# First attention of a two-layer transformer kernel: one pass of scores, with probability rows scaled, turned on TensorE and copied, in place of a second pass over keys

## The chip, the cores and the metric

The kernel runs on one core of a Trainium2 chip. The metric is the device time of one execution in microseconds (us), the median of several. The engines are TensorE (PE in the profile; its weight loads are PEld), VectorE (DVE), ScalarE (ACT), GpSimd (POOL) and SyncE (SP, which here issues all DMAs). They run their own instruction queues in order and meet at semaphores.

## The reference

A batch of 16 sequences of 512 tokens and 128 features goes through two layers. All of it is f32. Both layers have attention and an FFN in parallel on the same input.

```python
# layer 0 attention: 16 heads of 64, ALiBi slopes, causal
q, k, v = split(x @ w_qkv)
sim = einsum('bhid,bhjd->bhij', q * 64 ** -0.5, k)
sim = sim - abs(j - i) * slopes[h]
sim = where(causal, mask_value, sim)
attn = softmax(sim, axis=-1)
out = (attn @ v) @ w_out + b_out
# layer 0 and 1 FFN: LayerNorm twice, dequantised 128 -> 512 -> 128, GELU-like gate, residual
# layer 1 attention: differential, 16 sub-heads of 8, RoPE, no mask, per-head RMS norm
```

## The kernel before

The work of one batch element is cut into **ticks**; a **body** is 32 ticks, and in every body 8 pairs of heads of the first attention are started, one every 4 ticks (a **step**). The other parts of an element hang on a table of tick numbers (`X_AT` to `OUT_AT`, lines 98 to 111), counted from the element's first tick; an element lives for more than three bodies, so a body works on several elements at once. `pipeline` (line 528) writes bodies -1 to 2, a hardware loop of 12 turns over one body for elements 3 to 14, and bodies 15 to 17. Each engine has its own `body` that lists its instructions tick by tick; no engine waits for a tick, they only wait on semaphores, so a queue runs ahead or behind as its semaphores allow.

**First attention**, for a pair `p` of heads `j` = 0, 1, one on each half of the partitions. TensorE projects q, k and v (`project_q` and its like); ScalarE and VectorE split q and k into a high and a low f32r part (`QH`, `QL`, `KH`, `KL`). `max_scores0` (line 1325) makes the scores with queries on partitions, one 128-row block `q` per tick, three matmuls for each head. VectorE's `row_max0` (line 1071) adds the relative positions and the mask (`relkey`), takes the row maximum into `mx0` and throws the sum itself away (`junk`). A tick set later (`pair(s, 1)`) the maxima are turned (`minus_max`, line 1322), split by ScalarE (line 807) and VectorE (line 1042), and SP copies them by four small DMAs into rows of `QM` (line 571). Then `key_scores0` (lines 1358, 1361) makes the same scores again with **keys** on partitions: three matmuls for the products, one for positions and maxima (`KM`, `QM`), and two bf16 matmuls for the mask (`maskb`), for each head and block of keys. ScalarE's `exp0` (line 854) takes the exponential into `pt`. `pv0` (line 1375) multiplies with v; ScalarE copies the result into `att` (line 831). GpSimd adds the blocks of `pt` (`add_probs`, lines 703 and 707); every second step `sums0` (line 1384) sums them over partitions, ScalarE copies (line 838), SP spreads them over partitions (line 580), VectorE inverts (line 1080), SP writes them to HBM and reads them back as a broadcast into `rbc` (lines 585, 591), and GpSimd multiplies `att` by it (`normalise`, line 715). `attention_out` (line 1394) follows twice per element.

**Second attention** runs from tick `L1_AT` in 45 chunk steps over 28 ticks. `rotate` (VectorE, lines 1093 to 1105) makes three bf16 parts of q and of k; SP's `stack` writes them to HBM (line 600), 64 partitions at a time, and reads them back as stacks (line 606), which `s_stk` reports. Scores with queries on partitions (line 1442) give maxima on VectorE (line 1125), which go as rows through SP (line 615); scores with keys on partitions (line 1435) give exponentials on ScalarE (line 877), and line 1404 multiplies with v.

**Banks.** All score tiles of both attentions (`mx0`, `st0`, `mx1`, `st1`) take turns in five PSUM banks in the order that `score_order` writes down; before it writes a bank, TensorE waits until the tile that was there five places earlier has been read (`bank_free`): by VectorE for `mx0` and `mx1`, by ScalarE for `st0` and `st1`. All other TensorE results take turns in two banks (`pj_order`).

## Time and profile before

| | |
|---|---|
| median of 3 runs | 3957.96 us (3951.04 to 3959.59) |
| profiled execution | 3963.12 us, of which the span from first to last instruction is 3961.3 us |
| TensorE busy | 3169.1 us (80%), 20864 matmul records, mean granted clock 0.873 |
| VectorE busy | 2004.2 us (51%) |
| ScalarE busy | 1558.8 us (39%) |
| GpSimd busy | 1073.6 us (27%) |
| DMA | 105.81 MB, 27 GB/s on average |

Matmul ends are modelled, and a record lasts longer than the distance to the next one, so costs in a dense row of matmuls are read from start to start. In a view of waits "issue" means that the profile shows nothing that the engine waited for.

### The profile page before, as it was taken

To read this page: it belongs to the slowest core of one execution; us is meant where nothing else is said; L and a number is where in the kernel's file an instruction comes from. 1 tells how busy PE (TensorE), PEld (TensorE's weight loads), DVE (VectorE), ACT (ScalarE), POOL (GpSimd) and SP (SyncE) were. 2 spreads that over 40 slices of the span, in tenths; PEclk is the share of its full clock that TensorE was granted. 3 is DMA by queue.
4 is the path that set the end of the run, shared out by engine and by line. 5 is a ranking of instruction groups with operands and counts; after the bars stand their busy time and mean duration, and the time that the engine had idled before them with its cause. 6 is when DMAs were issued, how large, how long until landed. Compare 5 with 4: busy or idle time off the path is not lost. (4 is left out here: it accounts for less than half of the span.)

```text
span 3961.3 us, 67447 instructions
## 1 busy us (share of the span) xinstructions
PE 3169.1 (80%) x20864; PEld 1662.4 (42%) x20864; DVE 2004.2 (51%) x5450; ACT 1558.8 (39%) x3241; POOL 1073.6 (27%) x1482
## 2 busy tenths in 40 slices
PE   4877878788787887878878788787878878788767
PEld 2544444444444444444444344443444444444422
DVE  3345455455545554554555555545545555455455
ACT  2433434334343343534434344343443434344344
POOL 1432232323223232232322313222132231323120
PEclk9998889888798888988989889888988989889886
DMA  2010020100101001010010101101010020100120
GB/s 65 18 39 20 10 47 13 42 16 15 41 16 41 13 15 41 16 47 8 20 37 16 47 8 39 24 10 47 8 47 16 10 47 13 44 13 13 41 46 4
DMA packets 102986, 105.81 MB, mean 27 GB/s; under 512 B 35524, under 2 KB 81988, under 8 KB 99404
## 3 DMA queue, kind: packets, MB, share of 16 engines
q1 hardware_dynamic: 102604, 101.07, 10.6%
q8 instruction: 196, 3.21, 0.3%
q14 instruction: 186, 1.52, 0.1%
HBM read 68.77 MB, written 29.88 MB: 25 GB/s over the span
## 5 line engine op out<-in xcount | busy, mean ns | idle before, releaser
L1125 DVE TENSOR_REDUCE mx<-sc 128x1 f32<-128x512 f32 x1024 | 642.4, 679 | 251.7 <-PE sc L1442 250.8
L854 ACT ACTIVATE pt<-sc 128x512 f32<-128x512 f32 (+3 forms) x1024 | 392.2, 435 | 765.9 <-PE sc L1361 764.9
L877 ACT ACTIVATE pt<-sc 128x512 f32<-128x512 f32 x1024 | 555.8, 602 | 340.4 <-PE sc L1435 339.9
L1071 DVE CUSTOM_DVE_ANT_0 junk<-sc,relkey 128x128 bf16<-128x128 f32 (+3 forms) x1024 | 464.3, 487 | 370.0 <-PE sc L1337 236.0
L1442 PE MATMUL sc<-KS,QS 48*128 48x512 bf16 x1024 | 287.1, 433 | 317.7 <-issue 187.1
L703 POOL COPY psums<-pt 128x128 f32<-128x128 f32 x256 | 74.7, 295 | 1331.2 <-ACT pt L854 1331.0
L1276 PE MATMUL pj<-xnT,wqkv 128*128 128x512 f32 x512 | 376.3, 826 | 44.5 <-ACT y L800 37.6
L707 POOL TENSOR_TENSOR psums<-psums,pt 128x256 f32<-128x256 f32 (+1 forms) x512 | 306.8, 622 | 334.8 <-ACT pt L854 334.8
L707 POOL TENSOR_TENSOR psums<-pt 128x384 f32<-128x384 f32 x256 | 252.3, 1007 | 507.8 <-ACT pt L854 506.6
L1435 PE MATMUL sc<-QS,KS 51*128 51x512 bf16 x1024 | 262.7, 415 | 133.7 <-DVE mx L1071 109.6
L1358 PE MATMUL sc<-QH,KH 64*128 64x256 f32 (+2 forms) x1024 | 281.6, 434 | 89.1 <-DVE mx L1071 54.6
L1375 PE MATMUL pj<-pt,v 128*64 128x512 f32 (+3 forms) x2048 | 351.4, 489 | 0.6
L1404 PE MATMUL op<-pt,v 128*32 128x512 f32 x2048 | 318.1, 697 | 31.1 <-ACT pt L877 30.2
L1375 PEld LDWEIGHTS pj<-pt,v 128*64 128x64 f32 x2048 | 151.1, 153 | 310.4 <-issue 271.5
L1337 PE MATMUL sc<-KH,QH 64*128 64x256 f32 (+2 forms) x1024 | 258.8, 453 | 23.4 <-DVE mx L1125 20.6
L1442 PEld LDWEIGHTS sc<-KS,QS 48*128 48x128 bf16 x1024 | 68.2, 96 | 493.8 <-issue 233.8
L1028 DVE SCALAR_TENSOR_TENSOR y<-tanh,y 128x512 f32<-128x512 f32 x128 | 95.2, 744 | 336.5 <-ACT y L800 336.3
L819 ACT ACTIVATE KH<-pj 128x512 fp32r<-128x512 f32 x128 | 76.4, 597 | 466.7 <-PE pj L1276 465.7
L1358 PEld LDWEIGHTS sc<-QH,KH 64*128 64x128 f32 x1024 | 134.1, 195 | 263.1 <-DVE mx L1125 100.7
L1435 PEld LDWEIGHTS sc<-QS,KS 51*128 51x128 bf16 x1024 | 64.9, 95 | 420.0 <-issue 200.8
L1358 PE MATMUL sc<-QL,KH 64*128 64x256 f32 (+2 forms) x1024 | 217.1, 352 | 0.0
L1358 PE MATMUL sc<-QM,KM 64*128 64x256 f32 (+2 forms) x1024 | 204.9, 340 | 0.0
(130 smaller groups left out, 5195.5 us busy)
## 6 DMA issues: line engine op xcount, KB each, us to landing
rbc<-scr_r SPq DMA_DIRECT2D x128, 256.0 KB, 4.0
scr_p<-y SPq DMA_DIRECT2D x320, 64.0 KB
QS<-scr_p SPq DMA_DIRECT2D x32, 384.0 KB, 6.1
KS<-scr_p SPq DMA_DIRECT2D x32, 384.0 KB, 5.5
QM<-mrow SPq DMA_DIRECT2D x512, 2.0 KB
QS<-nrow SPq DMA_DIRECT2D x384, 2.0 KB
x_in<-in_L_attn_x SPq DMA_DIRECT2D x16, 256.0 KB, 2.8
scr_p<-tanh SPq DMA_DIRECT2D x64, 64.0 KB
```

Source lines behind the costliest of these rows:

```text
L707: pool.tensor_tensor(psums[:, c, P * k:T], so_far, tile, ALU.add).then_inc(s_psum, 1)
L854: act.activation(pt[:, base + OFFS[k]:base + OFFS[k] + WIDTH[k]], sc[tile_bank("st0", m)][:, c0:c0 + WIDTH[k]], ACT.Exp, scale=SLOPES[2 * ...
L877: act.activation(pt1[:, GS * (m % 2) + 2 * j + h, :], sc[tile_bank("st1", 2 * n + h)][:, :], ACT.Exp, scale=float(DS) ** -0.25).then_inc(s ...
L1071: dve.tensor_tensor_reduce(out=junk[:, m % 2, 0:width], in0=sc[tile_bank("mx0", m)][:, 0:width], in1=relkey[:, T - width:T], scale=1.0, sc ...
L1125: dve.reduce_max(mx1[:, g % 2, at:at + 1], sc[tile_bank("mx1", 2 * t + h)][:, :], AXIS.X).then_inc(s_mxd1, 1)
L1276: last = pe.matmul(t[:, c * k:c * (k + 1)], w(k), x(k), start=True, stop=True)
L1337: last = pe.matmul(sc[tile_bank("mx0", m + j)][:, 0:width], x[r, b, P * q:P * (q + 1)], y_[r, b, 0:width], start=c == 0, stop=c == 2)
L1358: pe.matmul(t[:, 0:T - q0], x, z, start=c == 0, stop=False, skip_group_check=True)
L1375: last = pe.matmul(t[DH * j:DH * (j + 1), P * k:T], v0[:, p % NBUF, k, DH * j:DH * (j + 1)], pt[:, base:base + WIDTH[k]], start=k == 0, st ...
L1404: last = pe.matmul(op[32 * j:32 * (j + 1), :], v1[:, k, (GS * g + j) // 2, :], pt1[:, GS * (k % 2) + j, :], start=k == 0, stop=k == NT - 1)
L1435: pe.matmul(sc[tile_bank("st1", 2 * m + h)][:, :], KS[r, slot, P * k:P * (k + 1)], QS[r, slot, :], start=True, stop=True).then_inc(s_st1, 1)
L1442: pe.matmul(sc[tile_bank("mx1", 2 * t + h)][:, :], QS[r, slot, P * q:P * (q + 1)], KS[r, slot, :], start=True, stop=True).then_inc(s_mxf1, 1)
```

## The change

The keys-on-partitions pass of the first attention goes (`key_scores0`, `maskb`, `KM`, `QM`, `minus_max`, `max_rows`), and so do the sums by GpSimd and TensorE, the trip of the inverse sums through HBM and the final `normalise`. In their place:

- `row_max0` keeps what it made: the operation writes the scaled scores with positions and mask as f32 rows into `pq` (with the sign turned, so that its minimum is minus the maximum).
- `exp0` works in place on these rows, query block by query block, with the minimum as bias, and sums each row (`accum_out`).
- VectorE's `invert_sums` inverts the 8 columns of sums of a pair; GpSimd's `scale_probs` multiplies the 8 row blocks of a pair by them.
- `turn_probs` transposes the 10 blocks of 128x128 per head on TensorE into score tiles `tr0`, three tiles per head with 4, 3 and 3 blocks; ScalarE's `copy_turned` copies each tile into `pt`.
- `pv0` stands one step later than before, and its copy is already normalised.

`QH` to `KL` have 2 buffers for 4. There is no loop any more: all 19 bodies are written out. The tick table is new, several parts of an element have ticks of their own on the engine that finishes them (`HID0_AT`, `ADDA_AT` and their like), the steps of the second attention in a tick are set in two halves between the first attention's parts, and its parts are stored by one DMA over 128 partitions for two over 64; the three rows of maxima go by 3 DMAs for 6. The diff, cut to its core:

```diff
-FIRST_LOOPED, LAST_LOOPED = 3, NB - 2
...
-X_AT = -24
-LN0_AT = (-13, -12, -10)
-XNT0_AT, HT0_AT = -6, -3
-FFN0_AT, FA_AT = 0, 5
-WOA_AT, WOB_AT = 28, 42
-LN1_AT = (42, 43, 45)
-XNT1_AT = 44
-ROPE_AT = (45, 46)
-STACK_AT = (48, 50)
-VALS_AT, HT1_AT = 50, 51
-L1_AT, L1_TICKS = 52, 28
-FFN1_AT, FB_AT = 53, 58
-TAIL_AT = 80
-OT_AT, OUT_AT = 83, 84
+
+X_AT = -22
+LN0_AT = (-14, -12, -10)
+XNT0_AT = -6
+HT0_AT = -2
+FFN0_AT = (1, 2, 4, 6)
+FA_AT = 10
+WOA_AT = 34
+WOB_AT = 46
+LN1_AT = (47, 48, 50)
+XNT1_AT = 49
+ROPE_AT = (50, 51)
+STORE_AT = (56, 57)
+STACK_AT = (56, 58)
+VALS_AT = 54
+HT1_AT = 54
+L1_AT = 58
+L1_TICKS = 28
+FFN1_AT = (56, 57, 59, 60)
+FB_AT = 63
+TAIL_AT = 86
+TURN3_AT = 87
+OT_AT = 90
+OUT_AT = 91
+HID0_AT = (4, 4, 8, 8)
+HID1_AT = (59, 59, 61, 62)
+ADDA_AT = 12
+ADDB_AT = 64
+ADDWA_AT = 36
+ADDWB_AT = 46
+TURN_ROPE_AT = (51, 52)
+HEAD3A_AT = 88
+HEAD3B_AT = 89
+ADDOUT_AT = 92
+PLN0_AT = (-13, -10)
+PLN1_AT = (48, 49)
+RES0_AT = -8
+RES1_AT = 52
+HEAD3P_AT = 89
+STOREOUT_AT = 94
...
-ROWS_AT = 1
-KEY_LAG = GU + 5
-HEADS_AT = GU + 1
-TURN_AT = GU + 4
-NORM_LAG = 3
+ROWS_AT = 2
+KEY_LAG = 13
+HEADS_AT = 9
+TURN_AT = 10
+SCALE_LAG = 3
+NORM_LAG = 4
+NA_LAG = 0
...
+    def turned(s, lag, g):
+
+        p, ago = pair_at(s, lag)
+        order.append(("tr0", ago, 6 * p + g))
+
+    for n in range(TICKS):
+        s, r = divmod(n, 4)
+        if r == 0:
+            turned(s, 2, 2)
+            second(n, 0)
+            turned(s, 2, 3)
+            tops(s, 0, 0)
+            second(n, 1)
+            tops(s, 0, 1)
+        elif r == 1:
+            turned(s, 2, 4)
+            second(n, 0)
+            turned(s, 2, 5)
+            second(n, 1)
+        elif r == 2:
+            tops(s, 0, 2)
+            second(n, 0)
+            second(n, 1)
+            tops(s, 0, 3)
+        else:
+            turned(s, 1, 0)
+            second(n, 0)
+            turned(s, 1, 1)
+            second(n, 1)
...
-            for b in range(-1, FIRST_LOOPED):
-                body(Seq(b))
-            with engine.Fori(0, LAST_LOOPED - FIRST_LOOPED + 1) as j:
-                body(Seq(FIRST_LOOPED, j))
-            for b in range(LAST_LOOPED + 1, NB + 2):
+            for b in range(-1, NB + 2):
...
+            def store_parts(i, w):
+
+                stack_used = ready(i.upto(64, 0))
+                for c in range(3):
+                    part_there = ready(i.upto(6, 3 * w + c + 1))
+                    if w == 0 and c == 0:
+
+                        hold(sp, s_stk, stack_used)
+                    sp.wait_ge(s_part, part_there)
+                    for slot in PART_SLOTS[w][c]:
+                        rows = scr_p[w, DS * slot:DS * (slot + 1)]
+                        sp.dma_start(rows.rearrange("d s t -> s d t"), parts[w][c]).then_inc(s_pst[w], 16)
...
+                for r in range(3):
+                    rows = QS[STACK + r:P:HALF, 2 * g:2 * g + 2, :]
+                    sp.dma_start(rows.rearrange("o s (c f) -> o (s c) f", f=P), nrow[:, r, :]).then_inc(s_nd[g % 2], 16)
...
+            def scale_probs(i, p, q):
+
+                    m = 8 * p + 2 * q + j
+                    at = PT0 * (2 * (p % NROWS) + j) + ROW_OFF[q]
+                    rows = pq[:, at:at + P * (q + 1)]
+                    inverse_there = i.upto(NPAIR, p + 1)
+                    inverse_there = inverse_there if i.j is None else pool.to_reg(inverse_there)
+                    pool.wait_ge(s_pset, N_PSET)
+                    pool.wait_ge(s_rc, inverse_there)
+                    pool.tensor_scalar(rows, rows, rsum[:, p % NROWS, 2 * q + j:2 * q + j + 1], None, ALU.mult).then_inc(s_scl, 1)
...
+            def exp0(i, p, q):
+                    m = 8 * p + 2 * q + j
+                    at = PT0 * (2 * (p % NROWS) + j) + ROW_OFF[q]
+                    c = 2 * q + j
+                    rows = pq[:, at:at + P * (q + 1)]
+                    act.wait_ge(s_mxd0, i.upto(L0N, m + 1))
+                    act.activation(rows, rows, ACT.Exp, scale=-1.0, bias=mx0[:, p % NROWS, c:c + 1],
+                                   accum_out=lsum[:, p % NROWS, c:c + 1]).then_inc(s_exp0, 1)
+
+            def copy_turned(i, p, g):
+
+                j, c = divmod(g, 3)
+                m = 6 * p + g
+                base = PT0 * (2 * (p % 2) + j)
+                n = TURN_OFF[c + 1] - TURN_OFF[c]
+                if g == 0:
+
+                    before, was = (i, p - 2) if p >= 2 else (i.ago(1), p - 2 + NPAIR)
+                    if before.live():
+                        b, u = pj_use(before, f"pv{was}")
+                        act.wait_ge(s_pjf[b], u)
+                act.wait_ge(s_tr, i.upto(N_TURN, m + 1))
+                act.activation(pt[:, base + TURN_OFF[c]:base + TURN_OFF[c + 1]], sc[tile_bank("tr0", m)][:, 0:n],
+                               ACT.Copy).then_inc(s_ev, 1)
...
-                            copy_attention(old, p2)
+                        p, i = b.pair(s, 2)
+                        if i is not None:
+                            copy_turned(i, p, 2)
+                        p, i = b.pair(s, -1)
+                        if i is not None:
+                            split_q(i, p)
+                        second_attention(b, n, 0)
+                        p, i = b.pair(s, 2)
+                        if i is not None:
+                            copy_turned(i, p, 3)
+                        p, i = b.pair(s, -1)
+                        if i is not None:
+                            split_k(i, p)
+                        second_attention(b, n, 1)
+                        p, i = b.pair(s, 0)
+                        if i is not None:
+                            exp0(i, p, 0)
+                        others(b, n)
+                        p, i = b.pair(s, 3)
+                        if i is not None:
+                            copy_attention(i, p)
+                        p, i = b.pair(s, 2)
+                        if i is not None:
+                            copy_turned(i, p, 4)
                     elif r == 1:
-                        if nxt is not None:
-                            values(nxt, ps_)
-                        p3, old = b.pair(s, 3)
-                        if old is not None and s % 2 == 1:
-                            copy_sums(old, p3 // 2)
-                        second_attention(b, n)
-                        if i is not None:
-                            exp0(i, p, 0)
+                        second_attention(b, n, 0)
+                        p, i = b.pair(s, 2)
+                        if i is not None:
+                            copy_turned(i, p, 5)
+                        others(b, n)
+                        second_attention(b, n, 1)
...
+                    dve.tensor_tensor_reduce(out=pq[:, at:at + width], in0=sc[tile_bank("mx0", m)][:, 0:width],
+                                             in1=relkey[:, T - width:T], scale=-SLOPES[2 * p + j], scalar=-MASKED,
+                                             op0=ALU.add, op1=ALU.min, accum_out=mx0[:, p % NROWS, c:c + 1]).then_inc(s_mxd0, 1)
+
+            def invert_sums(i, p):
+
+                dve.wait_ge(s_exp0, i.upto(L0N, 8 * p + 8))
+                dve.reciprocal(rsum[:, p % NROWS, :], lsum[:, p % NROWS, :]).then_inc(s_rc, 1)
...
+            def turn_probs(i, p, g):
+
+                j, c = divmod(g, 3)
+                m = 6 * p + g
+                if g == 0:
+                    pe.wait_ge(s_scl, i.upto(L0N, 8 * p + 8))
+                bank_free(i, "tr0", m)
+                t = sc[tile_bank("tr0", m)]
+                for k in TURNED[c]:
+                    for q in range(k, NT):
+                        at = PT0 * (2 * (p % NROWS) + j) + ROW_OFF[q] + P * k
+                        to = OFFS[k] - TURN_OFF[c] + P * (q - k)
+                        last = pe.transpose(t[:, to:to + P], pq[:, at:at + P], ident[:, :])
+                last.then_inc(s_tr, 1)
...
-                            pv0(older, p2)
+                        p, i = b.pair(s, 2)
+                        if i is not None:
+                            turn_probs(i, p, 2)
+                        second_attention(b, n, 0)
+                        p, i = b.pair(s, -1)
+                        if i is not None:
+                            project_q(i, p)
+                        p, i = b.pair(s, 2)
+                        if i is not None:
+                            turn_probs(i, p, 3)
+                        p, i = b.pair(s, -1)
+                        if i is not None:
+                            project_k(i, p)
+                        p, i = b.pair(s, 0)
+                        if i is not None:
+                            max_scores0(i, p, 0)
+                        others(b, n)
+                        second_attention(b, n, 1)
+                        p, i = b.pair(s, 0)
+                        if i is not None:
+                            max_scores0(i, p, 1)
+                    elif r == 1:
+                        p, i = b.pair(s, 3)
+                        if i is not None:
+                            pv0(i, p)
+                        others(b, n)
+                        p, i = b.pair(s, 2)
+                        if i is not None:
+                            turn_probs(i, p, 4)
+                        second_attention(b, n, 0)
+                        p, i = b.pair(s, 2)
+                        if i is not None:
+                            turn_probs(i, p, 5)
+                        second_attention(b, n, 1)
```

The orders of the two functions `body` not shown in full: VectorE has `row_max0` of blocks 0, 1 and 2, 3 at ticks 0, 1, 1 and 3 of a step, and `invert_sums` of the pair before at the end of tick 0; GpSimd has `scale_probs` of the pair before at ticks 2 and 3, after the small work of the tick; ScalarE has `exp0` of blocks 0 to 3 at ticks 0, 2, 3 and 3, and `copy_turned` 0 and 1 at tick 3.

## Rows read from the trace of the kernel before

**Rows 1.** Stage windows: an unrolled body, a looped one; busy us of each engine.
```profile
core 0: us, PE busy (x) PEld busy (x) DVE busy (x) ACT busy (x) POOL busy (x), PEclk, DMA share, GB/s
417.50:657.60 240.10, 198.34 (x1305) 103.69 (x1304) 124.57 (x340) 96.90 (x202) 66.98 (x94) 0.87 0.11 26
1257.00:1503.00 246.00, 200.64 (x1307) 104.35 (x1305) 125.35 (x343) 97.21 (x203) 66.90 (x94) 0.86 0.11 26
```
**Rows 2.** The same view, three steps of one body; the second attention starts in the first.
```profile
1745.60:1784.00 38.40, 22.90 (x135) 12.17 (x136) 19.29 (x51) 9.53 (x20) 11.35 (x17) 0.77 0.29 67
1784.00:1813.20 29.20, 25.06 (x148) 15.35 (x147) 14.46 (x37) 8.38 (x17) 5.59 (x8) 0.78 0.01 1
...
1970.70:1987.80 17.10, 16.00 (x137) 10.47 (x133) 8.88 (x35) 8.36 (x20) 9.46 (x13) 0.99 0.28 70
```
**Rows 3.** TensorE's waits: who waited for whom, us in total, times, longest us.
```profile
PE sc L1442 <- issue: 187.1, 16, 13.2
PE sc L1435 <- DVE mx L1071: 109.6, 73, 3.8
PE sc L1442 <- DVE mx L1071: 75.7, 118, 2.3
PE sc L1358 <- DVE mx L1071: 54.6, 71, 4.2
...
PE pj L1322 <- issue: 37.0, 11, 3.9
```
**Rows 4.** Timeline of the DMA queue and TensorE: start us, us, instruction, count [idle before].
```profile
1974.74 6.43 SPq L600 DMA_DIRECT2D scr_p<-y  x10
1981.29 1.20 SPq L600 DMA_DIRECT2D scr_p<-tanh  x2
1985.53 0.81 SPq L606 DMA_DIRECT2D QS<-scr_p  x2
...
1995.86 0.78 SPq L606 DMA_DIRECT2D KS<-scr_p  x2
...
2002.81 0.61 PE L1442 MATMUL sc<-KS,QS 48*128 48x512 bf16 x2 [13.16 <-issue]
```
**Rows 5.** Timeline of TensorE: key-pass blocks of 512 and 256 columns at full clock, and what follows.
```profile
2074.54 0.51 PE L1358 MATMUL sc<-QH,KH 64*128 64x512 f32 x2
...
2075.74 0.66 PE L1268 MATMUL pj<-ident,hn 128*128 128x128 f32 x4
...
2053.38 0.29 PE L1358 MATMUL sc<-QH,KH 64*128 64x256 f32 x2
...
2053.93 0.89 PE L1442 MATMUL sc<-KS,QS 48*128 48x512 bf16 x2
```
**Rows 6.** The same: four transposes at full clock; sums of two pairs.
```profile
1987.01 0.60 PE L1268 MATMUL pj<-ident,o 128*128 128x128 f32 x4
...
2070.38 1.06 PE L1384 MATMUL pj<-psums,ones 128*32 128x512 f32 x8
```
**Rows 7.** Timeline of VectorE: the third part of k.
```profile
1965.99 0.69 DVE L1105 TENSOR_TENSOR tanh<-y 128x512 bf16<-128x512 f32 x1
```
**Rows 8.** ScalarE's groups by line and shape: busy us, mean ns | idle before.
```profile
L854 ACT ACTIVATE pt<-sc 128x512 f32<-128x512 f32 x256 | 139.3, 598 | 153.8 <-PE sc L1361 153.8
L854 ACT ACTIVATE pt<-sc 128x384 f32<-128x384 f32 x256 | 111.6, 488 | 226.4 <-PE sc L1361 226.4
```
**Rows 9.** GpSimd's groups on the page, busy us, mean ns.
```profile
L703 POOL COPY psums<-pt 128x128 f32<-128x128 f32 x256 | 74.7, 295 | 1331.2 <-ACT pt L854 1331.0
...
L707 POOL TENSOR_TENSOR psums<-psums,pt 128x256 f32<-128x256 f32 (+1 forms) x512 | 306.8, 622 | 334.8 <-ACT pt L854 334.8
L707 POOL TENSOR_TENSOR psums<-pt 128x384 f32<-128x384 f32 x256 | 252.3, 1007 | 507.8 <-ACT pt L854 506.6
L715 POOL TENSOR_TENSOR att<-att,rbc 128x512 f32<-128x512 f32 x128 | 159.8, 1269 | 16.8 <-DMA rbc<-scr_r 16.8
```
**Rows 10.** Timeline of TensorE: one `pv0` of a pair, behind the hole of Rows 4.
```profile
2005.99 3.72 PE L1375 MATMUL pj<-pt,v 128*64 128x512 f32 x16
```

806 lines of the change are left out of this document (337 added, 469 removed).

## The prediction

> **What bounds the kernel now.** I read first the stage windows. In one whole body of 32 ticks (246 us) TensorE is busy 200.6 us, VectorE 125.4, ScalarE 97.2 and GpSimd 66.9, at a granted clock of 0.86 [rows 1]. TensorE is the engine to shorten, and the body has 45 us in which it stands still. The steps of four ticks inside a body differ: the one without second attention is nearly solid (16.0 of 17.1 us, clock 0.99), while the two behind the second attention's start run at 22.9 of 38.4 and 25.1 of 29.2 us with the clock at 0.77 and 0.78 [rows 2]. The second view is who TensorE waits for [rows 3]. Three things are to be seen. A wait marked "issue" before line 1442 comes 16 times, once for each batch element, 187.1 us in all: it is `s_stk`, the stacks of the second attention, as the DMA queue shows [rows 4]. A wait marked "issue" before line 1322 comes 11 times, 37.0 us: eleven is the number of back edges of a loop of 12 turns, and line 1322 is the first TensorE work of a body. The rest are waits of 1 to 2 us for row maxima (VectorE frees a score bank) and evictions: the three largest, for lines 1435, 1442 and 1358, come to 239.9 us. So TensorE's queue sets the pace, with small holes that the order of work makes, and one big hole.
>
> **A: TensorE's work.** Out go, per pair of heads, the four key-pass blocks of lines 1358 and 1361. From the start of a block to what follows it, that of 512 columns takes 1.20 and one of 256 takes 0.55 us at full clock [rows 5]; the one of 384 lies between, 0.87, and there are two of 256: 3.17 us. Out goes half of `sums0` (8 records in 1.06 us for two pairs, so 0.5 us [rows 6]) and the small transpose of the maxima (0.1 to 0.3 us). That is 3.9 us, 31 us for the 8 pairs of a body, and 36 us when stretched by the body's clock of 0.86. In come 20 transposes of 128x128 f32 per pair. Four in a row take 0.60 us [rows 6]; a fifth would start some 0.44 to 0.49 us after the first if the last one's end sticks out as the others' do, so 0.11 to 0.12 us each, and I take 0.11; 160 are 17.6 us, 20.5 at the body's clock. Net -16 us; I take -17, as the gaps in front of line 1358 go too. Bounds: if every transpose costs 0.17 us (half clock, or a bank wait in each group) the gain is 8 us; at most it is 20. Times 16 elements: -272 us (-128 to -320).
>
> **B: the stacks.** In the DMA queue [rows 4] the first part store goes at 1974.7, in line behind `max_rows`, although VectorE has written even the last key part at 1966.7 [rows 7]. Then come 12 stores in 7.7 us, a landing of 3.0 (1982.5 to 1985.5), two loads, 12 stores again, a landing, two loads that end at 1996.6, and TensorE starts at 2002.8, 6.2 later, with 13.2 us of standing still behind it. After the change each part is stored by one DMA over 128 partitions: 6 issues of some 0.6 us, 3.7 us, for each of query and key, and `max_rows`, `spread_sums` and `inverse` are off the queue. The queries' stores are free to go as soon as the parts are there; what stays after the previous second attention ends is two loads (0.8 us), key stores (3.7), a landing (3.0), two loads (0.8) and their landing (6.2): 14.5 us. In the old tick table that stretch is also four ticks, 17.1 us [rows 2], and in the new one some 15 us. So the hole closes, just. I take -165 of the 187 us; bounds 0 (a store over 128 partitions might be as slow as two over 64) and -187. What is late next there is the queue itself, so part of the hole may come back as the ticks get shorter. The minus-max rows go from 6 to 3 DMAs a group, which pays for the lag of 3 steps in place of 4: nothing.
>
> **C: no loop.** The 11 waits of 3.4 us at the back edge go: -37 us. The price of code that is never repeated is seen in the body before the loop, which is unrolled already: 240.1 us against 246.0 for a looped one, same busy times [rows 1]. So unrolling costs nothing that these rows show. The Trainium skill ("Runtime: NRT & Kernel Launch", Instruction fetch mechanics) says that straight code is fetched ahead and a taken branch out of the window stalls; the trace agrees with its 3.4 us.
>
> **D: the other engines.** ScalarE gains per pair six evictions of the turned tiles, 512, 384 and 384 columns for each head: 2 x (0.60 + 0.49 + 0.49) = 3.16 us by the rows of line 854 [rows 8], and loses half of a 512-column copy (`copy_sums`), 0.30, and the small line 807, under 0.3. The eight exponentials keep their widths but read SBUF and also sum; what a sum costs ScalarE is not shown: between 0 and a third of a 0.6 us operation, 8 x 0.2 us, and I take 0.7. So +3.3 us per pair, 26 per body: 97 + 26 = 123 us. VectorE's row operation writes f32 in place of bf16, from PSUM as before, in the same widths: taken as no change, and 5 us of the body's 125 at most; eight reciprocals for four and no line 1042 leave it at 125 us. GpSimd loses 794 us (74.7 + 306.8 + 252.3 + 159.8, lines 703, 707, 715 [rows 9]), 50 per body, and gains 64 scalings. Not shown for these widths: bounded by the two-input operations, 2 x (2 x 622 + 1007 + 1269) = 7.0 us a pair, where 622 is the mean of 128 and 256 columns, and by half of that, 3.5 us, since there is one input (the copy of 128 columns takes 295 ns); I take 5.5, nearer to the adds. 17 + 44 = 61 us. All three stay under the 205 us that a body would then have. On the path the scalings stand between `invert_sums` (end of tick 4) and the first transposes (tick 7): two ticks, 12 us, and in the step without second attention 7 us, so they hide, by 1.5 us in the tightest place. If that cover is gone it costs TensorE 1.5 us per body.
> The chunks set in two halves, the FFN gates that VectorE takes up a tick or more after TensorE made them (`HID0_AT`, `HID1_AT`), and 240 score tiles a body for 256 touch the small waits. Of the 240 us of the three maxima rows [rows 3] I take off half, -120, and -40 for a clock that falls less (0.77 in the steps behind the hole, over 67 us a body). Bounds -350 and +200: new waits can take their place, since ScalarE has a quarter more to do and still frees the banks of two of four kinds of score tiles.
>
> **Tail.** The second attention starts 6 ticks later and the result leaves 10 ticks later: outside the steady part, ticks of 3 to 4 us, +20 (0 to +40).
>
> **Sum.** -272 - 165 - 37 - 160 + 20 = -614 us. The profiled execution took 3963.1 us (span 3961.3 and 1.8 around it), so 3349; the runs' median is 5.2 lower, which gives 3344, and I say 3345, a ratio of 0.845.
>
> **Rivals.** (1) TensorE's saved time turns into holes, because VectorE (125 us) and now ScalarE (123) pace the banks in the busy steps: half of A, B and C stay, D is nothing: 3958 - 136 - 165 - 37 + 20 = 3640. For it: 240 us of waits on maxima. Against: those two are busy half the time. (2) The new order closes the small waits too: D at -350, 3155. For it: the solid steps show what is possible. (3) The clock. The rows show it at 0.77 where TensorE had stood still and at 0.99 in a solid step [rows 2]; if it stays near 0.77 the 181 us of work a body become 205, +24 x 16 = +384: 3730. The Trainium skill ("TensorE: Matmul & The Clock Gate", Part 4) says that transposes don't count as work that holds the clock up, and here 2560 of some 16,600 TensorE instructions would be transposes. In the trace the transposes stand in fours among matmuls, at either level, so it can't tell. (4) Slower. ScalarE's queue has `copy_attention` of the pair three steps back at tick 0, but TensorE's `pv0` for it comes only at the start of tick 1. ScalarE stands there with the evictions of tr0 and st1 tiles queued behind, and TensorE, when through, waits for their banks. Serial, that is pv0 (16 records in 3.7 us [rows 10]), the copy of 0.6 and two exponentials of 1.2: 5.5 us in each of 128 steps, against 614/128 = 4.8 saved; from 4.8 on it is a loss, and at 5.5 it gives 4050. Against: this is pv0 at a low clock, and five banks hold some work meanwhile. (5) The time doesn't move, holes for work one to one.
>
> **Chances.** Forecast 0.54, (1) 0.17, (2) 0.13, (3) 0.08, (4) 0.06, (5) 0.02. Range 3090 to 3700: it takes in the forecast, (1) and (2) with their bounds, and leaves out 0.16. A measurement tells 0.2% (8 us) from no change: faster 0.92, same 0.02, slower 0.06.
>
> **What would show it.** A: TensorE's busy time per body near 180 us, transposes 0.11 us apart. B: no wait over 3 us before the second attention's first scores; if it stays near 11, B is wrong. C: no wait of 3 us once a body. D: ScalarE near 123, GpSimd near 61 us a body, no wait of transposes for GpSimd. Clock at or over 0.87 against (3); ScalarE's wait before `copy_attention` and what TensorE waits for behind it decide (4). The prediction is wrong if the body is over 225 or under 190 us.

## The result: 3009 us for 3959, below the range

The changed kernel takes 3009.3 us, median of 4 runs (3003.6 to 3016.5), against 3958.8 for the kernel before (3951.0 to 3960.8), a ratio of 0.7605 with a 95% interval of 0.7586 to 0.7625. The forecast was 3345 with a range from 3090 to 3700. The direction was right, but the size was wrong by a third: 949 us went and 614 were forecast. The profiled execution took 3003.6 us, its span 3001.8.

First the page's line of busy times, then two whole bodies of 32 ticks in the stage windows. They answer to rows 1.

```profile
PE 2676.3 (89%) x16640; PEld 1416.4 (47%) x16640; DVE 1893.4 (63%) x5381; ACT 1974.5 (66%) x4835; POOL 1396.4 (47%) x1353
```
```profile
core 0: us, PE busy (x) PEld busy (x) DVE busy (x) ACT busy (x) POOL busy (x), PEclk, DMA share, GB/s
1152.50:1330.30 177.80, 165.59 (x1044) 87.79 (x1040) 117.64 (x337) 122.84 (x303) 86.81 (x84) 0.98 0.09 22
1330.30:1506.40 176.10, 164.10 (x1044) 87.65 (x1040) 117.76 (x336) 122.71 (x303) 86.84 (x84) 0.99 0.09 22
```

A body takes 177 us where a looped one took 246, under the 190 that the prediction itself named as its sign of being wrong. TensorE is busy 165 of it, with 12 us of standing still where there were 45, at a clock of 0.98 where it was 0.86.

The fall of the span by 959.5 us can be split with three numbers of each profile. TensorE's busy time fell by 492.8 us (3169.1 to 2676.3), and the rest of the span by 466.7 (792.2 to 325.5). Busy time times the mean granted clock is roughly the work at full speed: 2767 us before, 2596 after, so 171 us less. This is an estimate, since the mean clock is over the whole span. The other 322 us of busy time are then the same work at a faster clock. So **171 us are work, 322 clock, 467 standing still**. Weighing each busy stretch of TensorE with the clock granted in it gives nearly the same: 2782 and 2601 us, so 181 of work and 312 of clock. The forecast had 272 in the first of these and only 40 in the second.

TensorE's waits, answering to rows 3 (us in total, times, longest us):

```profile
PE pj L1301 <- DVE xn L1031: 40.0, 2, 39.3
PE pj L1309 <- DVE y L1099: 35.8, 14, 2.9
PE sc L1381 <- POOL pq L696: 35.4, 23, 5.6
PE sc L1381 <- ACT pt L844: 23.4, 46, 1.8
...
PE sc L1453 <- DVE mx L1131: 12.2, 29, 1.4
PE sc L1381 <- DVE mx L1078: 11.8, 16, 2.9
PE sc L1453 <- DVE mx L1078: 9.4, 42, 0.2
...
PE sc L1453 <- issue: 3.3, 1, 3.3
```

The first row is the start of the kernel. The hole of 187 us is one wait of 3.3 us. All of TensorE's waits for VectorE's maxima together came to 339.7 us before, of which the three rows of 239.9 are a part [rows 3]; now they come to 53.6, and the three rows of the block hold 33.4 of them. The wait at the back edge is gone, and in its place stands one of 2.5 us once a body, for VectorE's `rotate` (L1099). The stores and stack loads of one element are seen in the DMA queue, answering to rows 4 (start us, us):

```profile
1325.57 3.16 SPq L610 DMA_DIRECT2D scr_p<-y  x5
1328.77 0.61 SPq L610 DMA_DIRECT2D scr_p<-tanh  x1
1343.87 0.81 SPq L620 DMA_DIRECT2D QS<-scr_p  x2
1344.72 3.11 SPq L610 DMA_DIRECT2D scr_p<-y  x5
1347.88 0.61 SPq L610 DMA_DIRECT2D scr_p<-tanh  x1
1353.52 0.78 SPq L620 DMA_DIRECT2D KS<-scr_p  x2
```

Six stores take 3.8 us to issue, the queries' ones are away 15 us before their stack is read, and the stack of the keys is read 9.7 us after that of the queries.

The new parts on GpSimd and ScalarE by shape, answering to rows 8 and 9 (busy us, mean ns of one | idle before):

```profile
L696 POOL TENSOR_SCALAR pq<-pq,rsum 128x512 f32<-128x512 f32 x256 | 399.9, 1573 | 0.0
L696 POOL TENSOR_SCALAR pq<-pq,rsum 128x384 f32<-128x384 f32 x256 | 315.1, 1242 | 0.0
...
L696 POOL TENSOR_SCALAR pq<-pq,rsum 128x128 f32<-128x128 f32 x256 | 157.1, 624 | 932.9 <-DVE rsum L1085 932.9
```
```profile
L844 ACT ACTIVATE pt<-sc 128x384 f32<-128x384 f32 x512 | 249.8, 492 | 160.6 <-PE sc L1381 159.0
L828 ACT ACTIVATION_READ_ACCUMULATOR pq<-pq,mx 128x1 f32 x1024 | 204.3, 200 | 0.0
L828 ACT ACTIVATE pq<-pq,mx 128x512 f32<-128x512 f32 x256 | 182.7, 725 | 0.0
```

The transposes on TensorE's timeline, answering to rows 6 (start us, us):

```profile
1308.38 0.60 PE L1381 MATMUL sc<-ident,pq 128*128 128x128 f32 x4
1308.81 1.02 PE L1309 MATMUL pj<-xnT,wqkv 128*128 128x512 f32 x2
```

Four transposes take 0.43 us from their start to the next instruction's, 0.11 each as taken.

### The profile page after: what moved, and what is told of

Read it like the earlier page. It is cut to its first block, busy times and chain, and to the rows that moved or that the text cites. A ratio compares the mean times of both kernels' runs of the same rounds, so it can differ in the third digit from the quotient of the medians.

```text
span 3001.8 us, 49523 instructions
## 1 busy us (share of the span) xinstructions
PE 2676.3 (89%) x16640; PEld 1416.4 (47%) x16640; DVE 1893.4 (63%) x5381; ACT 1974.5 (66%) x4835; POOL 1396.4 (47%) x1353
## 4 chain that ended last, share of the span: by engine, by line
PE 64%; ACT 13%; DVE 10%; POOL 6%; issue 5%; SPq 1%; DMA 1%; DVEq 0%; POOLq 0%; ACTq 0%
PE pj L1309 14%; PE sc L1364 10%; PE pj L1393 9%; PE op L1415 7%; PE sc L1381 7%; ACT pq L828 4%; PE pj L1324 4%; PE pj L1405 4%; PE sc L1453 3%; POOL pq L696 3%; PE sc L1446 3%; ACT pt L844 3%; ACT pt L866 2%; DVE mx L1131 2%; PE pj L1301 2%
## 5 line engine op out<-in xcount | busy, mean ns | idle before, releaser
L696 POOL TENSOR_SCALAR pq<-pq,rsum 128x128 f32<-128x128 f32 (+3 forms) x1024 | 1099.1, 1092 | 932.9 <-DVE rsum L1085 932.9
L1078 DVE CUSTOM_DVE_ANT_0 pq<-sc,relkey 128x128 f32<-128x128 f32 (+3 forms) x1024 | 457.9, 484 | 462.9 <-PE sc L1364 458.0
L844 ACT ACTIVATE pt<-sc 128x384 f32<-128x384 f32 (+1 forms) x768 | 401.7, 529 | 315.1 <-PE sc L1381 313.6
L828 ACT ACTIVATE pq<-pq,mx 128x128 f32<-128x128 f32 (+3 forms) x1024 | 565.9, 561 | 15.8 <-DVE mx L1078 13.4
L1381 PE MATMUL sc<-ident,pq 128*128 128x128 f32 x2560 | 431.5, 289 | 73.9 <-POOL pq L696 35.4
L1381 PEld LDWEIGHTS sc<-ident,pq 128*128 128x128 f32 x2560 | 287.1, 143 | 366.3 <-issue 188.9
L1364 PEld LDWEIGHTS sc<-KH,QH 64*128 64x128 f32 x1024 | 123.4, 186 | 312.3 <-issue 238.6
L828 ACT ACTIVATION_READ_ACCUMULATOR pq<-pq,mx 128x1 f32 x1024 | 204.3, 200 | 0.0
L1364 PE MATMUL sc<-KH,QL 64*128 64x256 f32 (+2 forms) x1024 | 201.1, 335 | 0.0
L1364 PE MATMUL sc<-KL,QH 64*128 64x256 f32 (+2 forms) x1024 | 187.0, 321 | 0.0
```

Of the source, the lines that this page charges most:

```text
L696: pool.tensor_scalar(rows, rows, rsum[:, p % NROWS, 2 * q + j:2 * q + j + 1], None, ALU.mult).then_inc(s_scl, 1)
L828: act.activation(rows, rows, ACT.Exp, scale=-1.0, bias=mx0[:, p % NROWS, c:c + 1], accum_out=lsum[:, p % NROWS, c:c + 1]).then_inc(s_exp0, 1)
L844: act.activation(pt[:, base + TURN_OFF[c]:base + TURN_OFF[c + 1]], sc[tile_bank("tr0", m)][:, 0:n], ACT.Copy).then_inc(s_ev, 1)
L1078: dve.tensor_tensor_reduce(out=pq[:, at:at + width], in0=sc[tile_bank("mx0", m)][:, 0:width], in1=relkey[:, T - width:T], scale=-SLOPES[2 ...
L1364: last = pe.matmul(sc[tile_bank("mx0", m + j)][:, 0:width], x[r, b, P * q:P * (q + 1)], y_[r, b, 0:width], start=c == 0, stop=c == 2)
L1381: last = pe.transpose(t[:, to:to + P], pq[:, at:at + P], ident[:, :])
```

## The experiments

All experiments ran with three rounds beside the kernel before. A number such as "-52" is the difference of medians to the kernel that the experiment was made from. Where the two come from different comparisons, their ratios to the kernel before are the fairer measure. Times 3958.8 us they give numbers up to 10 us away: -108 for -118 at b_five, -97 and -180 for -89 and -174 at b_nomax and b_nosums, +194 for +186 at a_hole. No reading hangs on that but the one of a_noscale, where it is said. Their names: `b_` is made from the kernel before, `a_` from the changed one.

### Parts of the change put on the kernel before, one at a time

**b_noloop**: no loop.

```diff
-            for b in range(-1, FIRST_LOOPED):
-                body(Seq(b))
-            with engine.Fori(0, LAST_LOOPED - FIRST_LOOPED + 1) as j:
-                body(Seq(FIRST_LOOPED, j))
-            for b in range(LAST_LOOPED + 1, NB + 2):
+            for b in range(-1, NB + 2):
                 body(Seq(b))
```

> The kernel before with all 19 bodies written out and nothing else changed. Theory (term C of the prediction): the 11 waits of 3.4 us at the back edge go and nothing else moves, so -37 us, near 3921. Rival: the loop costs more than that, because waits against register values and their arithmetic slow every queue in all 12 looped bodies; then -100 us or more. A second rival is that straight code is fetched too slowly and eats the gain: within 8 us of before.

Measured: 3900.9, ratio 0.9873 (0.9834 to 0.9912), -52. The mechanism of term C holds: the row of 11 waits is gone. It is larger than their 37 us. In the profiled executions TensorE stands still 38 us less and is busy 28 us less, at a clock of 0.877 for 0.873.

**b_stores**: each part is stored by one DMA over 128 partitions.

```diff
-                        for h in range(2):
-                            rows = scr_p[w, h, DS * slot:DS * (slot + 1)]
-                            sp.dma_start(rows.rearrange("d s t -> s d t"), parts[w][c][HALF * h:HALF * (h + 1), :]).then_inc(s_pst[w], 16)
+                        rows = scr_p[w, DS * slot:DS * (slot + 1)]
+                        sp.dma_start(rows.rearrange("d s t -> s d t"), parts[w][c]).then_inc(s_pst[w], 16)
```

> The kernel before with the parts of the second attention stored by one DMA over 128 partitions in place of two over 64 (12 stores an element fewer), all else as it was. Term B alone, as far as the store count makes it: 12 issues of 0.61 us leave the chain in front of the second attention, 7.3 us of a hole of 11.7, so -117 us, near 3841, and a hole of 4 us. If the clock follows the holes, the two steps behind it (0.77 in the kernel before) speed up as well: -150 to -200. Rival: a store over 128 partitions takes as long to issue or land as two over 64: no gain.

Measured: 3875.3, 0.9803 (0.9761 to 0.9844), -78, where -117 was expected. The hole went down by 75.6 us, and the time by as much:

```profile
PE sc L1442 <- issue: 111.5, 16, 7.9
```

**b_warm**: ten f32 matmuls of constants, 128x512, ahead of the wait for the stacks, so that TensorE does not stand still in the hole.

```diff
+                        hold(pe, s_or, i.upto(NG, 0))
+                        for _ in range(10):
+                            pe.matmul(op[:, :], wqkv[:, 0:P], wqkv[:, 0:T], start=True, stop=True)
                         pe.wait_ge(s_stk, i.upto(64, 64))
```

> The kernel before with ten more f32 matmuls of 128x512 per element (constant operands, results never read), placed on TensorE just in front of the wait for the stacks, so that it works through most of the 11.7 us in which it stood still. They lie in a wait and delay nothing but the last of it. Theory: the low clock behind the hole (0.77 over 67 us per element) comes from TensorE standing still in it; with it busy the clock there is 0.9 or more and the body gets 6 to 8 us shorter, -100 to -130 us, near 3840. Rival: the clock is low there because of the sparse steps themselves, not the hole: no gain, or up to +30 us for matmuls that stick out.

Measured: 3953.8, 0.9989 (0.9971 to 1.0008), no change. The hole is filled, as its timeline shows (start us, us, in brackets the idle time before):

```profile
1006.51 8.75 PE L1423 MATMUL op<-wqkv 128*128 128x512 f32 x20
1018.83 0.61 PE L1445 MATMUL sc<-KS,QS 48*128 48x512 bf16 x2 [3.57 <-DMA KS<-scr_p]
```

The hole's waits fall from 187.1 to 53.4 us. The mean clock went from 0.873 to 0.894, but what was gained lay within the filler. Over the 16 elements the granted clock of the 15 us ahead of the second attention's first scores rose from 0.68 to 0.99, and that of the 67 us behind it only from 0.81 to 0.83. So the low clock of the steps behind the hole [rows 2] is hardly its after-effect.

**b_split**: the second attention's steps of a tick in two halves between the first attention's parts, on TensorE, ScalarE, VectorE and in both bank orders.

```diff
                     elif r == 2:
-                        second_attention(b, n)
+                        second_attention(b, n, 0)
                         if i is not None:
                             exp0(i, p, 1)
+                        second_attention(b, n, 1)
```

> The kernel before with the second attention's steps of a tick set in two halves between the first attention's parts on TensorE, ScalarE and VectorE, as the changed kernel has it, and nothing else changed. Theory: the small waits for row maxima and evictions (240 us on the three largest rows) come from runs of four score tiles that one engine must read while TensorE wants its next bank; halves take off 60 to 120 us, near 3870. Rival: the halves are not what closed these waits, the work that went from VectorE's and TensorE's queues is: within 20 us of before.

Measured: 3811.8, 0.9642 (0.9606 to 0.9678), -141. TensorE's waits for maxima fell by 61 us (339.7 to 278.5) and the rest of the span outside its busy time by 40. The larger part is clock: TensorE is busy 113 us less with the same instructions (3169.1 to 3055.9). The hole is as long as ever (195.2 us), and yet the clock of the 67 us behind it is 0.90 where it was 0.81.

**b_gates**: VectorE takes up an FFN gate one tick later than TensorE and ScalarE make it.

```diff
-                        if (i := b.at(n, FFN0_AT + f)) is not None:
+                        if (i := b.at(n, FFN0_AT + f + 1)) is not None:
                             ffn_dve(i, 0, f)
-                        if (i := b.at(n, FFN1_AT + f)) is not None:
+                        if (i := b.at(n, FFN1_AT + f + 1)) is not None:
                             ffn_dve(i, 1, f)
```

> The kernel before with VectorE's half of each FFN gate one tick later in its own list, nothing else changed. In the kernel before VectorE waits 336 us for ScalarE at these gates, and row maxima stand in line behind them. The four edits together gave -403 where three of them alone sum to -271. Theory: the gates alone are worth the difference, about -130, near 3820. Rival: the gates are worth little (under 40) and it is the edits that help one another.

Measured: 3850.2, 0.9754 (0.9708 to 0.9801), -100. The reason is in a view that the prediction did not read, **VectorE's own waits**. Of the kernel before:

```profile
DVE y L1028 <- ACT y L800: 336.3, 111, 5.3
DVE mx L1125 <- PE sc L1442: 250.8, 133, 13.7
DVE junk L1071 <- PE sc L1337: 236.0, 122, 5.0
DVE xacc L1035 <- PE pj L1394: 172.0, 32, 6.6
DVE QL L1050 <- ACT QH L813: 158.4, 123, 7.1
```

VectorE stood 336 us for ScalarE's half of the gates, with the row maxima that free TensorE's banks queued behind. One tick later the operand is there: 0.0 us are left in front of that line. Not all of the 336 us are won, for VectorE now stands longer elsewhere; its waits marked "issue" before `row_max0` were 127.8 us. Two lines of b_gates, by shape and from the waits:

```profile
L1028 DVE SCALAR_TENSOR_TENSOR y<-tanh,y 128x512 f32<-128x512 f32 x128 | 93.6, 732 | 0.0
```
```profile
DVE junk L1071 <- issue: 321.9, 170, 4.7
```

For TensorE the waits for maxima fell by 51 us (339.7 to 289.1), and its busy time by 79 at a faster clock. Of the changed kernel, VectorE's own waits:

```profile
DVE pq L1078 <- PE sc L1364: 458.0, 242, 5.8
DVE mx L1131 <- PE sc L1453: 281.3, 218, 7.7
DVE QL L1053 <- ACT QH L795: 112.7, 84, 9.6
DVE xacc L1046 <- PE pj L1405: 62.2, 16, 3.9
```

VectorE now waits mainly for TensorE's scores themselves, which is to say that it is ahead. It is busy 51% of the span before and 63% after; what differs is what it stands in front of.

### The parts together

**b_four** is all four at once, **b_five** also moves the stores of the parts ahead in SyncE's list, to the tick behind `rotate`:

```diff
                     for w in range(2):
+                        if (i := b.at(n, ROPE_AT[w] + 1)) is not None:
+                            store_parts(i, w)
                         if (i := b.at(n, STACK_AT[w])) is not None:
                             stack(i, w)
```

> The kernel before with four edits at once that leave its first attention as it is: no loop (-52 measured alone), stores over 128 partitions (-78 alone), the second attention in halves (-141 alone), and VectorE's half of each FFN gate one tick later than TensorE's and ScalarE's (not measured alone). Theory: the parts add up, so -271 and some -30 for the gates, near 3655; then some 650 us of the changed kernel's gain come with the new first attention and the new places in the tick table, far more than the 272 that the prediction gave to TensorE's work. Rival: closing waits raises the clock for everything, so they do more together than alone: under 3500.

> The four edits plus the stores of the parts moved ahead in SP's list, each right behind the tick that makes the parts, so that they no longer stand in line behind the copies of the maxima; the loads stay where they were. The four edits leave 110 us of the hole before the second attention. Theory: the stores of the query are out of the way and the hole closes, -80 to -110, near 3445. Rival: the loads themselves, which wait for the previous second attention's end, set it: under 30 us.

Measured: b_four 3544.0, 0.8960 (0.8930 to 0.8989), -403 where the four single ones sum to -371: they add up, and a little more. The expectation of 3655 still had some 30 us for the gates. b_five 3426.1, 0.8686 (0.8658 to 0.8714), another -118; the row of the stack's hole is gone from TensorE's waits, whose first three on maxima are these:

```profile
PE sc L1447 <- DVE mx L1081: 64.7, 29, 3.8
PE sc L1370 <- DVE mx L1081: 61.1, 111, 4.2
PE sc L1454 <- DVE mx L1081: 54.4, 115, 2.3
```

So 13.1% of the time, more than half of the whole gain, comes without any change to what the first attention computes.

### TensorE's work taken away and added

**b_key1** is b_five with three of the four f32 matmuls of each key-pass tile left out: two of the three products of q and k, and the one of positions and maxima. The probabilities are then not the reference's. Below, "the three products" means these three matmuls.

```diff
                 for c in range(6):
+                        if c in (1, 2, 3):
+                            continue
                         if c < 4:
```

> The kernel of the five edits with three of the four products of the key pass left out (it keeps one product and the mask for each block, all tiles, waits, exponentials and copies), so the first attention's probabilities are not the reference's. At full clock these products take 1.94 us a pair, 248 us in all. Theory (term A of the prediction: TensorE's work counts whole): -250 to -280 against the kernel of the five edits. Rival (doubling the transposes cost 127 for 282 us of work, 0.45 each): -110.

Measured: 3466.9, 0.8780 (0.8757 to 0.8803), +41. Some 248 us of TensorE's work, by the distances between these records at full clock, are gone (229 when its busy time is weighed with the granted clock), and the kernel is slower. The page's line, and the waits that were at 64.7, 61.1 and 54.4 us:

```profile
PE 2905.9 (84%) x17792; PEld 1423.0 (41%) x17792; DVE 2036.1 (59%) x5450; ACT 1562.3 (45%) x3241; POOL 1080.6 (31%) x1482
```
```profile
PE sc L1449 <- DVE mx L1081: 100.0, 44, 5.4
PE sc L1372 <- DVE mx L1081: 73.7, 137, 4.6
PE sc L1456 <- DVE mx L1081: 73.2, 118, 3.0
```

TensorE's busy time fell by only 46 us (2952.2 to 2905.9), because the granted clock fell from 0.944 to 0.886, and the rest of the span grew by 87. So of the 229 us of work 182 come back as time lost to the lower clock and 87 as standing still. Its waits for maxima rise from 221.5 to 333.6 us: TensorE comes to the next bank earlier and waits there for the same row maximum.

**a_turn2** issues each transpose of the changed kernel twice; **a_turnhalf** leaves out 4 of the 10 per head in 15 elements, with those blocks of the probabilities holding what was in the bank.

```diff
+                        pe.transpose(t[:, to:to + P], pq[:, at:at + P], ident[:, :])
                         last = pe.transpose(t[:, to:to + P], pq[:, at:at + P], ident[:, :])
```
```diff
                     for q in range(k, NT):
+                        if i.lo > 0 and (q - k) % 2 and k < 3:
+                            continue
                         at = PT0 * (2 * (p % NROWS) + j) + ROW_OFF[q] + P * k
```

> The changed kernel with every one of the 2560 transposes issued twice into the same place, the result as before. It prices TensorE's work in the changed kernel. Theory: TensorE is busy 165 of 177 us a body at nearly full clock, so it is the bound, and 2560 x 0.11 = 282 us come on top nearly whole, near 3280. Rival: other engines pace it and half of the work hides, near 3130. If transposes pulled the clock down, it would be over 3400 with a granted clock under 0.93.

> The changed kernel, with 4 of the 10 transposes per head left out for 15 of the 16 elements (those blocks of the probabilities keep what the bank held, so the output isn't the reference's). 960 transposes go, at 0.11 us 106 us of TensorE's work. If TensorE's own work sets the time of the changed kernel, as term A of the sum had it: 3009 - 106 = 2903, down to -0.11 x 960 at any clock. If the price found by doubling holds downwards as well (0.05 us each): -48, 2961. If TensorE's saved time turns wholly into holes: 3009 within 6 us.

Measured: a_turn2 3136.7, 0.794 (0.792 to 0.796), +127, or 0.050 us for each of 2560 transposes that lie 0.11 apart. a_turnhalf 2972.9, 0.7511 (0.7488 to 0.7534), -36, or 0.038 us for each of 960. In the changed kernel TensorE's work is worth some 35 to 45% of its length, up and down, a third to a half. The clock was 0.979 with twice as many transposes and 0.965 with fewer.

### The three side trips of the old key pass

**b_nomax** is b_five without the trip of the maxima (transpose, two splits, four small DMAs, the wait of the key pass), its exponential scaled by 1e-4 to stay finite. **b_nosums** is b_five without GpSimd's adds, the ones-matmuls and the trip of the inverse sums, the last scaling on 4 columns only. **b_keep** has both of these, and **b_strip** also lacks the three products of b_key1. None of the four computes the reference's probabilities. Two places of the edits, the first of b_nomax and the second of b_nosums:

```diff
-                if k == 0:
-                    pe.wait_ge(s_mdma[p % 2], i.upto(32 * NPAIR, 64 * (p // 2 + 1)))
...
-                        for k in ((), (0,), (1,), (2, 3))[r]:
-                            add_probs(i, p, k)
```

> The kernel before without its loop, with stores over 128 partitions moved ahead in the queue, halves and gates later (3426 us, ratio 0.869), and in it the trip of the maxima left out: no transpose, no split by ScalarE and VectorE, no four small DMAs, no wait of the key pass for them; the exponential is scaled by a ten-thousandth so that it stays finite, so the output isn't the reference's. If the remaining 417 us between it and the changed kernel hang on this chain: near 3200. If the chain is hidden and only its own instructions count (0.3 us of TensorE, 0.3 of ScalarE, 0.25 of VectorE a pair): -20 to -60, 3366 to 3406.

> The same 3426 us kernel with the sums left out instead: no adds by GpSimd, no ones-matmuls, no copy, spread, inverse, trip through HBM and broadcast; the last scaling works on 4 columns (the output isn't the reference's). TensorE loses 64 us of work. If work on TensorE counts whole: 3360. If GpSimd's adds hold probability tiles or the trip through HBM holds the end: near 3250. If all is hidden: 3426 within 10.

> The same 3426 us kernel with everything left out that the change removes from the first attention: three of four products of the key pass, the trip of the maxima, the sums and their trip (the output isn't the reference's). Nothing of what the change puts in is there, so on every engine it has less to do than the changed kernel. If the work taken out is what makes the remaining 417 us: under 3009. If it is the order of the work (the table of ticks and each engine's list) that the changed kernel has and this one hasn't: 3300 to 3450, with waits for VectorE's maxima ahead of the score matmuls over 250 us and the clock under 0.92.

> The 3426 us kernel without the trip of the maxima and without the sums and their trip, but with all four products of the key pass (the exponential scaled as before; the output isn't the reference's). Against the one that also lacks three of the four products (3192 us) it has 248 us more of TensorE's work at full clock. If TensorE's work sets the time: 3440. If, as in the other pair (3426 with the products, 3467 without), the work fills holes and the clock makes up the rest: 3150 to 3210, at a clock over 0.95 where the other had 0.915.

| | us | ratio | 95% interval | clock |
|---|---|---|---|---|
| b_five | 3426.1 | 0.8686 | 0.8658 to 0.8714 | 0.944 |
| b_nomax | 3336.9 | 0.8441 | 0.8413 to 0.8469 | 0.956 |
| b_nosums | 3252.4 | 0.8231 | 0.8202 to 0.8261 | 0.970 |
| b_keep | 3204.8 | 0.8094 | 0.8067 to 0.8122 | 0.969 |
| b_strip | 3192.2 | 0.8065 | 0.8031 to 0.8100 | 0.915 |

b_keep and b_strip are b_key1's question again on another ground, and the answer is the same: the three products are worth 12.6 us (11 by the ratios), within the intervals of the two, and the clock falls by 0.054 when they go. Their busy lines, b_keep's first:

```profile
PE 2817.3 (88%) x20224; PEld 1548.7 (48%) x20224; DVE 1880.9 (59%) x5258; ACT 1495.1 (47%) x3049; POOL 311.1 (10%) x458
```
```profile
PE 2754.7 (86%) x17152; PEld 1381.2 (43%) x17152; DVE 1874.3 (59%) x5258; ACT 1499.2 (47%) x3049; POOL 306.8 (10%) x458
```

The maxima and the sums together (b_keep) are worth 5.9%, 234 us, less than the two taken singly. The sums are the surprise. TensorE does at most 68 us of them (64 groups of 1.06 us [rows 6]), and 174 went. Part of the rest is that VectorE got faster, with nothing changed on it. By shape, two of its lines in b_five and then in b_nosums (busy us, mean ns):

```profile
L1038 DVE SCALAR_TENSOR_TENSOR y<-tanh,y 128x512 f32<-128x512 f32 x128 | 117.0, 914 | 0.0
...
L1030 DVE TENSOR_SCALAR hn<-xn,mv,rstd 128x128 f32<-128x128 f32 x128 | 59.2, 523 | 3.5 <-POOL rstd L675 3.5
```
```profile
L1030 DVE SCALAR_TENSOR_TENSOR y<-tanh,y 128x512 f32<-128x512 f32 x128 | 87.2, 681 | 0.0
...
L1022 DVE TENSOR_SCALAR hn<-xn,mv,rstd 128x128 f32<-128x128 f32 x128 | 39.4, 370 | 3.1 <-POOL rstd L672 3.1
```

In b_five the 74 operations of line 1030 that lie for over half their time beside one of GpSimd's adds take 701 ns on average, and the 179 that lie beside none take 359. Line 1038, with two inputs in SBUF, takes 1091 beside them and 821 otherwise (44 and 84). These blocks stand in VectorE's list ahead of row maxima. The Trainium skill ("SBUF — State Buffer", SBUF: two separate sides) says that GpSimd and VectorE share one pair of ports, which one of them holds for a whole instruction when VectorE's has two SBUF inputs or runs in a fast mode; the adds agree with it. The scalings of the changed kernel don't, for the operation with two SBUF inputs takes 671 ns beside them and 684 otherwise (47 and 66). Of the 175 us by which the profiled span fell, some 42 are TensorE's work, 82 clock and 51 standing still. How much of the last two comes from the faster VectorE was not measured apart.

### The changed kernel's own weak places

**a_hole**: the stack of the keys is loaded three times in a chain, so that the hole comes back.

```diff
-                for h in range(2):
+                for again in range(1 + 2 * w):
+                    if again:
+                        sp.wait_ge(s_stk, i.upto(128, 32 + 32 * again))
+                    for h in range(2):
```

> The changed kernel with the stacks of the keys loaded three times over in place of once, one load behind the other's landing, the same data each time: the second attention of each element may start some 13 us later than now. It puts back a hole before the second attention like the one that the kernel before had (11.7 us). In the changed kernel the loads of the element in the middle land at 1354.3 + 5.5 = 1360 us. Theory: a hole costs its own length and nothing for the clock, as the filled hole showed: between +100 and +190 us by what slack there is. Rival: in a kernel that TensorE bounds the clock lost behind the hole costs as much again: +250 us or more.

Measured: 3195.6, 0.8095 (0.8073 to 0.8118), +186, for this row of waits, and the clock at 0.942. TensorE's busy time grew by 31 us with the same instructions, and the clock of the 15 us behind the hole is 0.84 for 0.98: here the hole did cost some clock beside its length.

```profile
PE sc L1456 <- issue: 164.4, 16, 16.6
```

**a_noscale**: GpSimd's scalings on 4 columns, so that the probabilities are not divided by their sums.

```diff
-                    pool.tensor_scalar(rows, rows, rsum[:, p % NROWS, 2 * q + j:2 * q + j + 1], None, ALU.mult)
+                    pool.tensor_scalar(rows[:, 0:4], rows[:, 0:4], rsum[:, p % NROWS, 2 * q + j:2 * q + j + 1], None, ALU.mult)
```

> The changed kernel with GpSimd's 1024 scalings of probability rows cut to 4 columns each, so that the probabilities aren't normalised; all waits stay. The scalings take 1099 us, 8.6 us a pair, where the prediction took 5.5. TensorE's waits for them are 35 us. Theory: they hide, and only these waits go: -20 to -35 us. Rival: VectorE and GpSimd slow each other on their way to SBUF and the whole kernel gains: -80 us or more.

Measured: 2993.1, 0.7574 (0.7554 to 0.7594), -16, or -12 by the ratios, whose intervals overlap, though GpSimd's busy time went from 1396 to 585 us. 811 us of GpSimd's work hide but for that. TensorE's waits for the scalings went, and in front of the same line its waits for maxima grew from 11.8 to 46.6 us.

**a_late4**: on VectorE the third block's row operation moves from the end of tick 1 to the start of tick 2, and the LayerNorm, FFN and head parts of tick 2 come last, in the manner of the kernel before.

```diff
+                    elif r == 2:
                         p, i = b.pair(s, 0)
                         if i is not None:
                             row_max0(i, p, 2)
-                    elif r == 2:
+                        second_attention(b, n, 0)
+                        second_attention(b, n, 1)
                         others(b, n)
                         norms(b, n)
-                        second_attention(b, n, 0)
-                        second_attention(b, n, 1)
```

> The changed kernel with VectorE's list in tick 2 of each step put back to the manner of the kernel before: the third block's row operation at the start of tick 2 and not at the end of tick 1, and the layer norms, residual sums and gates of that tick behind the second attention's maxima and not ahead of them. Same work, other queues untouched. Theory: VectorE running ahead of TensorE is a part of what closed the small waits: +30 to +100 us. Rival: with five banks the place in the list makes no difference: within 8 us.

Measured: 3059.2, 0.7742 (0.7721 to 0.7763), +50 for the order of one tick in four, with the same work on every engine. The way is not the one of the expectation, though: TensorE's waits for maxima did not grow (53.6 us before, 50.9 now). It now waits twice as long for the scalings, which need VectorE's inverse sums:

```profile
PE sc L1381 <- POOL pq L696: 72.3, 28, 5.6
```

**a_loop**: the loop of 12 turns put back.

> The changed kernel with a loop of 12 turns over one body again. Put on the kernel before, writing out the loop gave 52 us. If that price belongs to the back edges (11, 3.4 us each, and what the clock loses behind them): 3009 + 37 to 52 = 3046 to 3061. If the changed order hides the back edge behind other engines' work: 3009 to 3020.

Measured: 3051.5, 0.7715 (0.7692 to 0.7737), +42. Term C is a term of its own in both kernels, 52 and 42 us. The waits at the back edge are shorter here; of the 47 us by which the profiled span grew 17 are standing still and 29 busy time at a lower clock (0.959 for 0.970):

```profile
PE sc L1385 <- issue: 15.1, 11, 1.7
```

### The ledger

In shares of the kernel before (3958.8 us), by the ratios: order, loop and queues alone, down to b_five, 13.1%, 520 us; the side trips of maxima and sums, to b_keep, 5.9%, 234 us; three of the four f32 matmuls of a key-pass tile, to b_strip, 0.3%, 11 us; and from b_strip to the changed kernel 4.6%, 182 us, although that last step also adds the transposes, the scalings and six evictions a pair. What is left there to gain it from is the rest of the key pass and the rest of the order: own ticks for what VectorE adds and normalises, the places of the row maxima, and 240 score tiles a body for 256. In b_strip TensorE still waits 263 us in five rows for VectorE's maxima, and VectorE 271 us for ScalarE's `QH` at the head of its list. Which of these moves makes the 182 us was not tried one by one, so that part stays open; a_late4 shows only that one such place weighs some 50 us.

The same by TensorE's time in the profiled executions, in us. "Work at full clock" is its busy time weighed with the granted clock, which can be off by 1% (order alone should not change it), and "lost to the clock" is what is left of the busy time:

| | busy | work at full clock | lost to the clock | not busy |
|---|---|---|---|---|
| before | 3169 | 2782 | 387 | 792 |
| b_split | 3056 | 2780 | 276 | 752 |
| b_gates | 3091 | 2805 | 285 | 750 |
| b_five | 2952 | 2789 | 164 | 470 |
| b_key1 | 2906 | 2560 | 346 | 557 |
| b_nosums | 2829 | 2747 | 82 | 419 |
| b_keep | 2817 | 2731 | 86 | 383 |
| b_strip | 2755 | 2508 | 247 | 434 |
| changed | 2676 | 2601 | 75 | 326 |

From the kernel before to b_five the work stays and the clock and the standing still fall together, by 223 and 322 us. Where only matmuls go, in b_key1 and b_strip, both rise again.

## Why the prediction came out as it did

**What bounds it.** "TensorE's queue sets the pace" was half true. TensorE was read as the bound because it was the busiest and because the small waits looked small. But with 792 us of standing still and a clock of 0.873 it was the engine that showed the damage. The chain of waits was followed one step, from TensorE to VectorE's maxima, and not the second, from VectorE to ScalarE's gates, where 336 us stood.

**A, work, -272.** The sizes were right: transposes 0.11 us apart, and by busy time times clock some 171 us of work less, in the bounds. The accounting was wrong. Work was counted whole, as path, and "stretched by the clock" on top. b_key1 (+41) and b_keep against b_strip (-13) show that the key pass's products had filled time that was there anyway, at a clock that fell when they went. What did give time was the side trips that A counted as 0.5 and 0.3 us a pair, or as nothing: -89 for the maxima and -174 for the sums, 234 for the two together. A also took the transposes at their full 0.11 us, where a_turn2 and a_turnhalf price them at 0.04 to 0.05. Between b_five and the changed kernel TensorE is busy 276 us less. That looks like A's 272, but 89 of it are clock.

**B, the hole, -165.** Right in mechanism and nearly in size. The row went from 187.1 to 3.3 us; b_stores gave 78, the earlier issue in b_five 118 (108 by the ratios), together 186 to 196, and a_hole took 186 for 164 us of hole. Both bounds of the store over 128 partitions are settled: 0.61 us to issue, as over 64. The tick table had to hide the rest, and it did: "So the hole closes, just." How close it was, no run shows.

**C, the loop, -37.** Right in mechanism, and 52 or 42 us in size, the more by the clock. The forecast that no wait of 3 us comes once a body holds by a little: one of up to 2.9 stands there.

**D, small waits and clock, -160.** This is the step that failed. "Of the 240 us of the three maxima rows [rows 3] I take off half, -120, and -40 for a clock that falls less." Both sizes fell short. TensorE's waits for maxima came to 339.7 us and not 240, and 286 of them went. The clock gave 312 to 322 us where 40 were taken. On the kernel before, the halves (-141) and the gates (-100) alone outdo the whole of D, and more than half of that is clock. A clock of 0.87 means that a quarter of the time is at the lower level, and 0.97 that 6% is. The low clock was put down to the hole ("the steps behind the hole"), and b_warm shows that filling the hole leaves it (0.83 for 0.81 in the 67 us behind it), while b_split raises it to 0.90 with the hole unfilled. As far as these runs show, it goes with the many short waits of those steps; where they closed, in b_split, b_gates, b_four and b_five, the clock rose each time (0.897, 0.900, 0.924, 0.944).

**Engines.** ScalarE 123 us a body as forecast, in a different mixture: reading the sums takes 200 ns each, 1.6 us a pair, and an exponential out of SBUF 725 ns for 512 columns where one from PSUM took 598 [rows 8]. VectorE 118 for 125. GpSimd 87 for 61: the scalings take 8.7 us a pair (2 x (0.624 + 0.928 + 1.242 + 1.573)), outside the bound of 7.0, which rested on the idea that one input can't be dearer than two [rows 9]. The idea that they hide was right (a_noscale, 12 to 16 us). "No wait of transposes for GpSimd" was wrong by 35 us in 23 waits.

**The rivals.** (1) holes for work, 3640, falls as a whole, but its rule was right for the key pass's products. (2), the order closes the small waits too, named the mechanism, and even its 3155 was 146 us too high: it had 350 us for small waits and clock together, and nothing for what the side trips held up. (3), the clock stays at 0.77, falls: 0.97. The Trainium skill ("TensorE: Matmul & The Clock Gate", Part 4) says that transposes don't count as work that holds the clock up. These runs speak against it: with 5120 transposes among 19,200 TensorE instructions (a_turn2) the clock was 0.979, and with 2560 among 16,640 it was 0.970. But the transposes stand in short groups among matmuls, so no run shows a long stretch of them alone. (4), slower through `copy_attention` at the head of ScalarE's tick: the wait is there, 1.9 us a pair, but so it was in the kernel before (272.7 us),

```profile
ACT att L818 <- PE pj L1393: 242.5, 128, 3.8
```

and TensorE's waits for ScalarE's `copy_turned` are only 23.4 us in all, so five banks hold enough work. (5) falls.

The range failed mainly because its lower end bounded the two terms that the trace did not size, waits and clock, by 350 us taken from the waits of one engine. The 182 us between b_strip and the changed kernel, whose moves were not tried singly, are a part of the miss that stays unexplained.

## What to carry over

When the busiest engine has many short waits for another, read that other engine's own waits before sizing anything: an operation at the head of its list that waits for a third engine holds every bank release behind it, and moving it by one tick cost nothing here and gave 100 us. Work of the busiest engine is worth its length only where nothing else comes last, so price it by leaving some out or doubling it, and expect a hole that is waited for whole, as for a DMA, to cost its own length, and here up to a fifth more by the clock. Gains of order add up and bring the clock back with them; a forecast should have a term for the clock, with what the low level costs as its bound: 387 us of TensorE's busy time in the kernel before, of which 312 came back.

## What the runs showed of the hardware

- Filling a hole of 13 us with matmuls of constants returned nothing (ratio 0.9989), and taking matmuls out of a dense stretch lowered the granted clock (0.944 to 0.886, 0.969 to 0.915): of 229 and 223 us of work taken out, 182 and 160 came back as time lost to the clock.
- GpSimd's multiplication by one factor per row took 624, 928, 1242 and 1573 ns for 128, 256, 384 and 512 f32 columns, more than its two-input multiplication of 512 (1269) or add of 384 (1007) [rows 9].
- Beside GpSimd's adds a VectorE operation with one SBUF input took 701 ns for 359. Beside the scalings of the changed kernel the same line took 460 for 356 (67 and 189 operations), and the one with two SBUF inputs was not slowed (671 for 684, 47 and 66), while beside the adds it was (1091 for 821).
- ScalarE's accumulated row sum is an instruction of its own, 200 ns.
